# Layer 2's attention in a four-layer kernel: queries and context reordered by channel, parts cut, stored and loaded earlier

## What is computed

```python
qh = q.reshape(b * h, d // h, m)        # h = 8, d = 128, m = 256
kh = k.reshape(b * h, d // h, -1)
vh = v.reshape(b * h, c // h, -1)
qk = jnp.einsum('bdm,bdn->bmn', qh, kh) * scale
sm = jax.nn.softmax(qk, axis=-1)
ret = jnp.einsum('bmn,bcn->bcm', sm, vh)
...
x = x + _L2_xattn_ref(_layernorm(x, axis=-1), ctx_2048, ctx_2048)
```

## Time and profile before

| what | value |
|---|---|
| median of 3 runs | 2378.38 us (2377.53 to 2382.86) |
| the profiled execution's own time | 2386.57 us |
| its span | 2384.8 us |
| PE busy | 2021.2 us (85%) |
| DVE busy | 1812.9 us (76%) |
| ACT busy | 1405.9 us (59%) |
| POOL busy | 1170.7 us (49%) |

### The profile page before, as it was taken

How to read it: one execution, slowest core, us unless ns; L and a number is a source line. 1 busy time by engine, 2 the same in 40 slices (tenths; PEclk the granted TensorE clock), 3 DMA queues, 4 the chain that set the end, 5 groups by cost and what they waited for, 6 DMA issues and landing times.

```text
span 2384.8 us, 42664 instructions
## 1 busy us (share of the span) xinstructions
PE 2021.2 (85%) x13467; PEld 1235.8 (52%) x13467; DVE 1812.9 (76%) x4024; ACT 1405.9 (59%) x3555; POOL 1170.7 (49%) x1397
## 2 busy tenths in 40 slices
PE   5999879999589999999999995794687667888787
PEld 2444355666267677677777774462343233333245
DVE  4899658475589999999998877664785996888464
ACT  0677621453278888888888882231366563777543
POOL 3444100442678888888888762334762122334100
PEclk9999769999799999999999996897699675999789
DMA  5566420786310000000110004333994113777200
GB/s 139 142 173 173 117 78 8 244 246 203 70 33 19 21 19 21 17 21 19 21 21 17 3 1 180 122 87 106 221 249 137 53 32 79 178 183 184 67 14 27
DMA packets 258181, 223.19 MB, mean 94 GB/s; under 512 B 36585, under 2 KB 237900, under 8 KB 257708
## 3 DMA queue, kind: packets, MB, share of 16 engines
q1 hardware_dynamic: 234668, 178.72, 27.5%
q0 software_dynamic: 12240, 32.39, 5.5%
q10 hardware_dynamic: 11056, 9.38, 1.3%
HBM read 141.98 MB, written 79.32 MB: 93 GB/s over the span
## 4 chain that ended last, share of the span: by engine, by line
PE 58%; DVE 17%; POOL 10%; issue 7%; ACT 5%; DMA 2%; SPq 1%; POOLq 0%; ACTq 0%; DVEq 0%
PE bank L3216 8%; PE bank L713 5%; PE bank L691 4%; PE bank L1534 4%; PE bank L3176 3%; PE bank L3165 3%; PE bank L3209 3%; PE bank L1547 3%; PE bank L2113 3%; PE bank L3152 3%; PE bank L3144 2%; PE bank L3197 2%; POOL f_hr L3536 2%; PE bank L754 1%; POOL f_rows L3518 1%
## 5 line engine op out<-in xcount | busy, mean ns | idle before, releaser
L3216 PE MATMUL bank<-f_w,f_zc 128*128 128x512 bf16 x1152 | 283.8, 383 | 22.2 <-DVE f_zc L3324 18.1
L3536 POOL TENSOR_TENSOR f_hr<-f_hr,half_pow 128x4 f32<-128x4 f32 x192 | 244.9, 1275 | 84.3 <-DVE f_hr L3333 84.1
L926 ACT ACTIVATE a_PT<-bank 128x512 f32<-128x512 f32 x384 | 214.6, 603 | 82.6 <-PE bank L698 74.0
L815 DVE TENSOR_REDUCE a_nm<-bank 128x2 f32<-128x512 f32 x384 | 243.0, 683 | 21.1 <-PE bank L691 20.4
L3428 ACT ACTIVATE f_Pm<-bank,f_nmax 128x128 f32<-128x128 f32 x512 | 183.0, 383 | 73.6 <-DVE f_nmax L3348 73.4
L691 PE MATMUL bank<-a_stack_k,a_stack_q 57*128 57x256 bf16 (+1 forms) x768 | 165.1, 299 | 70.5 <-DVE a_nm L815 41.7
L3216 PEld LDWEIGHTS bank<-f_w,f_zc 128*128 128x128 bf16 x1152 | 112.4, 99 | 122.2 <-issue 25.1
L926 ACT ACTIVATE f_w<-bank 128x512 f32<-128x512 f32 x256 | 141.2, 599 | 48.6 <-PE bank L698 37.2
L815 DVE TENSOR_REDUCE f_w<-bank 128x2 f32<-128x512 f32 x256 | 162.4, 680 | 9.5 <-PE bank L691 8.0
L3343 DVE TENSOR_TENSOR f_raw<-bank,f_hr 128x512 f32<-128x512 f32 x192 | 131.5, 685 | 42.7 <-POOL f_hr L3536 42.7
L3525 POOL TENSOR_TENSOR f_cf<-f_cbr,f_cmr 128x516 f32<-128x516 bf16 x128 | 157.0, 1227 | 12.6 <-DVE f_cb L3373 11.0
(11 more groups left out here) (406 smaller groups left out, 5221.1 us busy)
## 6 DMA issues: line engine op xcount, KB each, us to landing
o<-a_sums SPq DMA_DIRECT2D x32, 512.0 KB
cut<-a_parts SPq DMA_DIRECT2D x64, 192.0 KB
cut<-a_parts SPq DMA_DIRECT2D x96, 128.0 KB
m_w<-in_w SPq DMA_DIRECT2D x32, 368.0 KB
moe_out<-m_oe ACTq DMA_DIRECT2D x32, 256.0 KB
cut<-f_w SPq DMA_DIRECT2D x32, 192.0 KB, 3.5
cut<-f_w SPq DMA_DIRECT2D x48, 128.0 KB, 2.6
f_w<-cut SPq DMA_DIRECT2D x32, 192.0 KB, 3.6
```

The lines of the kernel that those rows point to most:

```text
L815: v.tensor_reduce(self.nm[:, g % 2, :, at % self.J, at // self.J], self.k.bank[h % 3][:, :].rearrange("p (n m) -> p n m", n=2), AX.X, ALU. ...
L926: a.activation(self.PT[:, h % 8, :, :].rearrange("p m n -> p (m n)"), self.k.bank[3 + h % 3][:, :], ACT.Exp).then_inc(self.a_exp.sem, 1)
L3216: x = t.matmul(ps[:, :], self.zc[:, b % 2, j, c_, :], self.fp8.w3[:, m, c_, at:at + BANK], start=(m == 0 and c_ == 0), stop=(m == 2 and c_ ...
L3536: g.tensor_tensor(f, f, self.k.half_pow[:, 0:self.HPB], ALU.pow).then_inc(self.g_hr.sem, 1)
```

## The change

- The 128 channels of layer 2's attention are reordered, so that all eight heads of one channel index stand side by side (channel d of head h at row 8d + h instead of 16h + d). ctx comes in that order from a second input array. The queries are brought into it by a matmul with a permutation matrix `order_q` (`R`, step 8b+5), and ACT copies the result from bank 7 to `QK` (`copy_R`, step 8b+6). DVE now writes the normalised queries to `xn`. `copy_V` puts V back in order of heads.
- The DRAM tensor `cut` of layer 2 is laid out as part, channel, position. A row of a stack is then 4 KB without a gap. Four DMAs store an element's parts instead of five, and of k three part planes are stored instead of six. Four DMAs load the stacks instead of two.
- ACT's first part moves from step 8b+13 to 8b+7, POOL's cutting from 8b+14 to 8b+7, the store from 8b+19 to 8b+11, and the load of elements 0 to 5 from 8b+27 to 8b+14.
- POOL clears the first four buffers of V ahead of step 0. The gathers of element 2, which stood in step 0, follow the first cutting; the others keep their places.

```diff
+
+    def loaded(self, t):
+
+        b = self.starts(t, 14)
+        if self.layer == 2 and b is not None and b < self.NST:
+            return b
+        b = self.starts(t, 27)
+        return b if self.layer != 2 or b is not None and b >= self.NST else None
...
             yield "V", self.starts(t, 0)
+        if self.layer == 2 and self.starts(t, 5) is not None:
+            yield "R", self.starts(t, 5)
         if self.layer == 0 and self.starts(t, 6) is not None:
...
         self.stats, self.mv = s("stats", [P, B, 6]), s("mv", [P, B, 4])
-        self.cut = k.nc.dram_tensor(f"cut_{layer}", (B, 2, P, 6, D), BF16, kind="Internal").ap()
+        self.cut = k.nc.dram_tensor(f"cut_{layer}", (B, 2, P, 6, D) if layer != 2 else (B, 2, 6, P, D), BF16, kind="Internal").ap()
         self.o_out = k.nc.dram_tensor(f"o_{layer}", (B, heads, 32, D), F32, kind="Internal").ap()
...
         self.v_var, self.g_pow, self.v_x, self.a_V = (claim(f"a_{n}", B) for n in ("v_var", "g_pow", "v_x", "a_V"))
+        self.a_R = claim("a_a_R", B * (layer == 2))
         self.g_qk = claim("a_g_qk", 2 * B * (layer == 0))
...
         loads = []
+        if self.layer == 2:
+            rows = self.cut[b].rearrange("w c (d s) n -> w (c d) s n", d=self.hd)
+            loads.append((self.stack_q[0:self.ROWS, i, :, :], rows[0]))
+            for at, n in ((0, 3), (3, 2), (5, 1)):
+                loads.append((self.stack_k[at * self.hd:(at + n) * self.hd, i, :, :], rows[1, 0:n * self.hd]))
+            return loads
         for w, stack in enumerate((self.stack_q, self.stack_k)):
...
         A, layer = self.k.A, self.layer
+        if layer == 2:
+            sp.dma_start(self.order_q[:, :], A["c_order"]).then_inc(self.d_par.sem, 16)
         if layer == 0:
...
         dst = self.QK[:, i, 1, :] if self.layer == 2 else self.ctx_t[:, i, :]
-        sp.dma_start(dst, self.k.A["ctx"][:, b, :]).then_inc(self.d_ctx[i].sem, 16)
+        src = self.k.A["ctx_by_channel" if self.layer == 2 else "ctx"]
+        sp.dma_start(dst, src[:, b, :]).then_inc(self.d_ctx[i].sem, 16)
     def store_cut(self, sp, b):
+
         i, d = b % self.NB, self.d_cut[b % self.NB]
         sp.wait_ge(self.g_p2.sem, self.g_p2.at(b + 1))
+        if self.layer == 2:
+            for at, n, w, c_, m in ((0, 3, 0, 0, 1), (3, 2, 0, 1, 1), (5, 1, 0, 2, 1), (0, 3, 1, 0, 3)):
+                src = self.parts[:, i, w, c_:c_ + m, :]
+                src = src.to_broadcast([P, n, D]) if n > m else src
+                sp.dma_start(self.cut[b, w, at:at + n].rearrange("c p n -> p c n"), src).then_inc(d.sem, 16)
+            return
         q, kk = self.parts[:, i, 0], self.parts[:, i, 1]
...
                 t.wait_ge(self.a_V.sem, self.a_V.at(at + 1))
+            elif what == "R":
+                t.wait_ge(self.a_R.sem, self.a_R.at(at + 1))
             else:
...
             x.then_inc(self.p_m.sem, 1)
+        if what == "R":
+            if at == 0:
+                t.wait_ge(self.d_par.sem, self.d_par.at(1))
+            t.wait_ge(self.v_x.sem, self.v_x.at(at + 1))
+            t.matmul(ps[:, 0:D], self.order_q[:, :], self.xn[:, i, :], start=True, stop=True).then_inc(self.p_m.sem, 1)
         if what in "XCQ":
...
             v.wait_ge(self.g_pow.sem, self.g_pow.at(at + 1))
-            if at >= self.NB and layer == 2:
-                v.wait_ge(self.g_p2.sem, self.g_p2.at(at - self.NB + 1))
-            if at >= self.NB and layer != 2:
-                v.wait_ge(self.p_m.sem, self.p_m.at(self.uses["X" if layer == 0 else "Q", at - self.NB] + 1))
-            dst = self.QK[:, i, 0, :] if layer == 2 else self.xn[:, i, :]
-            v.tensor_scalar(dst, X[:, at, :], m[:, 0:1], m[:, 3:4], ALU.subtract, ALU.mult).then_inc(self.v_x.sem, 1)
+            if at >= self.NB:
+                v.wait_ge(self.p_m.sem, self.p_m.at(self.uses[{0: "X", 2: "R", 3: "Q"}[layer], at - self.NB] + 1))
+            v.tensor_scalar(self.xn[:, i, :], X[:, at, :], m[:, 0:1], m[:, 3:4], ALU.subtract, ALU.mult).then_inc(self.v_x.sem, 1)
         for w, what, after in ((1, "C", 7), (0, "X", 10)):
...
             self.copy_V(a, self.starts(t, 1))
-        if self.starts(t, 13) is not None:
-            self.first_part(a, self.starts(t, 13))
+        if self.layer == 2 and self.starts(t, 6) is not None:
+            self.copy_R(a, self.starts(t, 6))
+        if self.starts(t, self.FIRST) is not None:
+            self.first_part(a, self.starts(t, self.FIRST))
         q = self.quad(t - 1)
...
             a.wait_ge(self.p_O.sem, self.p_O.at((b - self.NV + 1) * self.heads // 4))
+        if self.layer == 2:
+            a.copy(self.V1[:, i, :, :, 0:self.hd], ps[:, 0:D].rearrange("p (n d h) -> p n h d", n=2, h=self.heads)).then_inc(self.a_V.sem, 1)
+            return
         if self.layer != 3:
...
+    def copy_R(self, a, b):
+        i = b % self.NB
+        a.wait_ge(self.p_m.sem, self.p_m.at(self.uses["R", b] + 1))
+        if b >= self.NB:
+            a.wait_ge(self.g_p2.sem, self.g_p2.at(b - self.NB + 1))
+        a.copy(self.QK[:, i, 0, :], self.k.bank[7][:, 0:D]).then_inc(self.a_R.sem, 1)
+
     def first_part(self, a, b):
         i = b % self.NB
         if self.layer == 0:
             a.wait_ge(self.g_qk.sem, self.g_qk.at(2 * b + 2))
         if self.layer == 2:
-            a.wait_ge(self.v_x.sem, self.v_x.at(b + 1))
+            a.wait_ge(self.a_R.sem, self.a_R.at(b + 1))
             a.wait_ge(self.d_ctx[i].sem, self.d_ctx[i].at(b // self.NB + 1))
         if self.layer == 3:
             a.wait_ge(self.v_m.sem, self.v_m.at(self.by_dve["Q", b] + 1))
         if b >= self.NB:
-            a.wait_ge(self.d_cut[i].sem, self.d_cut[i].at(5 * (b // self.NB)))
+            a.wait_ge(self.d_cut[i].sem, self.d_cut[i].at(self.n_cut * (b // self.NB)))
         a.copy(self.parts[:, i, :, 0, :], self.QK[:, i, :, :]).then_inc(self.a_p0.sem, 1)
...
             g.tensor_tensor(m[:, 3:4], m[:, 2:3], k.half_pow[:, 0:1], ALU.pow).then_inc(self.g_pow.sem, 1)
-            if at < self.NV:
+            if at < self.NV and not (self.pairs and at < self.SOON):
                 self.clear_V(g, at)
-            if self.pairs and at == 0:
-                self.pairs.gather(g, 2)
         for w, what, after in ((1, "C", 8), (0, "X", 11)):
             at = self.starts(t, after)
             if at is not None and layer == 0:
                 g.wait_ge(self.v_m.sem, self.v_m.at(self.by_dve[what, at] + 1))
                 x, y = self.QK[:, at % self.NB, w, :], self.t1[:, at % self.NB, w, :]
                 g.tensor_tensor(x, x, y, ALU.add).then_inc(self.g_qk.sem, 1)
-        at = self.starts(t, 14)
+        at = self.starts(t, self.PARTS)
         if at is not None:
...
                             ALU.subtract).then_inc(self.g_p2.sem, 1)
-        at = self.starts(t, 15)
-        if at is not None and self.pairs and at + 3 < B:
-            self.pairs.gather(g, at + 3)
+        at = self.starts(t, 7)
+        if at is not None and self.pairs and at + 2 < B:
+            self.pairs.gather(g, at + 2)
         at = self.ended(t, self.SUM + 2)
...
     g["mask"] = m.reshape(-1)
+    by_channel = np.arange(P).reshape(8, 16).T.reshape(-1)
+    g["ctx_by_channel"] = np.ascontiguousarray(g["ctx"][by_channel])
+    g["c_order"] = np.ascontiguousarray(np.eye(P, dtype=np.float32)[by_channel].T)
     g["mask_T"] = np.ascontiguousarray(m.reshape(B, DC, P).transpose(2, 0, 1))
     g.update(more_arrays(a))
     g.update(constants())
```

More of the change, by code:

```diff
@@ L335 @@
     LEAD, TURNED, EXP, VALUES, SUM = 40, 21, 22, 24, 53
-    HEAD_BANK = 5
+    HEAD_BANK, SOON = 5, 4
     def __init__(self, k, layer, pairs=None, headed=False, tailed=False):
@@ L351, in __init__ @@
         self.NB = 2 if layer != 2 else 4
+        self.FIRST, self.PARTS, self.CUT = (13, 14, 19) if layer != 2 else (7, 7, 11)
         self.ctx = ExitStack()
@@ L466, in allocate_head @@
             self.m_out = k.nc.dram_tensor("mask_rows", (B, 2, self.MROWS, D), BF16, kind="Internal").ap()
+        if layer == 2:
+            self.order_q = s("order_q", [P, P])
         self.signals()
@@ L471, in signals @@
         last = lambda name, n, unit=1: claim(f"tail_{name}" if self.tailed else f"a_{name}", n, unit, own=self.tailed)
-        self.n_load = {0: 5, 2: 0, 3: 5 + self.heads}[layer]
+        self.n_load = {0: 5, 2: 1, 3: 5 + self.heads}[layer]
+        self.n_cut = 5 if layer != 2 else 4
         self.n_stack = len(self.loads(0))
@@ L478, in signals @@
         self.d_ctx = [claim(f"a_d_ctx{i}", B // self.NB, 16) for i in range(self.NB)]
-        self.d_cut = [claim(f"a_d_cut{i}", B // self.NB * 5, 16) for i in range(self.NB)]
+        self.d_cut = [claim(f"a_d_cut{i}", B // self.NB * self.n_cut, 16) for i in range(self.NB)]
         self.d_stack = [claim(f"a_d_stack{i}", B // self.NB * self.n_stack, 16) for i in range(self.NB)]
@@ L562, in sp_step @@
     def sp_step(self, sp, t):
-        b = self.starts(t, 19)
+        b = self.starts(t, self.CUT)
         if b is not None:
```

(8 more changed lines are left out.)

## The result

The changed kernel takes 2415.14 us (median of 4 runs, 2412.84 to 2417.64), the kernel before 2380.62 beside it (4 runs, 2377.53 to 2383.39): ratio 1.0151, 95% interval 1.0130 to 1.0172, so it is slower by 34.5 us in the medians. (Ratios here are those on record with their intervals; a quotient of two medians, here 1.0145, can differ from them by about 0.001.) The forecast was slower by 18.7, 2397, with a range up to 2412, and 2415.14 lies above that range. The sign was right, the size too small.

What follows compares the result with a forecast made beforehand. The prediction took POOL's rounds, with their waits for ACT's cast, to bound layer 2's attention. It summed 1.9 + 11.2 + 6 + 4.7 - 1.1 - 4 = +18.7 us, giving 2397 against the median 2378.38, range 2380 to 2412.

Steps and rivals of the forecast that it cites:

- What bounds the stage: Layer 2's attention: its length is the sum of POOL's rounds until cutting ends; POOL waited 29.0 us for ACT's first part.
- Start, +1.9: Ahead of the first power: four clears of V, about 0.78 us each, move that power by +1.9 us.
- Lead-in, +11.2: Power 0 to power 5: rounds of 9.42 us with R in the chain, 47.6 us against 36.4, +11.2.
- Power 5 to 9, +6: Four rounds: R, its copy and handoffs add 1.8 us each; taken as +6 us, bounds +3 and +7.2.
- Power 9 to 14, +4.7: Five rounds: floor 10.0 us from 8.09 plus 1.9, taken as 10.4 against 9.46, +4.7 us, bounds 0 and +9.7.
- End of cutting: After power 14: only element 15's cutting is left behind, 20.9 us against 22.1, term -1.1 us.
- relief: DVE's waits for reloaded sums: larger rows and smaller stores shorten the DMA queue, -4 us, bounds 0 and -4.8.
- estimate of 2 us: Alternative for the DMA saving: fixed packet overhead gives only 14% of the loads' time, -2 us instead of -4.
- The signs: Expected: lead-in rounds 9.4 us, waits 2.9, first scores near 1683; wrong if middle rounds exceed 12 or sums' waits stay.
- Absorbed: Rival for the middle rounds: existing slack hides the new chain, which costs only in the lead-in; +10.2, 2389 us, chance 0.14.
- PE at its lower level in the middle: Rival: longer waits at R drop PE's clock, up to +19 over five rounds; +33, 2411 us, chance 0.13.
- The DMA queue sets the middle: Rival: transfers pace rounds 5 to 14, which fall to 8.1 us with R hidden; -7, 2371 us, chance 0.07.

Runs made afterwards that it cites:

- e4: The changed kernel with POOL's cutting at step 14, behind the next element's power, stores at 15, first loads at 20; cast stays at 7: 2357.97 us, ratio 0.9915.
- e8: The kernel before with ACT's cast of layer 2 at step 7 instead of 13, nothing else changed: 2362.23 us, ratio 0.9929.
- e2: The changed kernel without R and its copy, so the queries' channels stay unsorted; DVE writes the normalised queries to QK: 2389.1 us, ratio 1.0049.
- e5: The changed kernel with all nine clears of V ahead of the first power instead of four: 2409.32 us, ratio 1.0135.
- e6: The changed kernel itself, unaltered, run and profiled again: 2410.48 us, ratio 1.0143.
- e7: e3 with one number changed, ACT's cast at step 5 instead of 7: 2377.18 us, ratio 0.9996.
- e3: The kernel before (old layout, no R) with the new steps, including those of first loads, clears and gathers: 2392.07 us, ratio 1.0057.
- e10: The steps of e4 on the new layout without R and its copy, queries' channels left unsorted: 2358.55 us, ratio 0.9911.
- e9: The steps of e4 on the old layout (512-byte rows) without R: 2359.63 us, ratio 0.9920.

## Why the prediction was right or wrong

**What bounds the stage: right.** The stage follows POOL's rounds, and the wait for ACT's cast decides them: of the 26.0 us that the stage grew, POOL's waits for the cast are 20.9. e4 and e8 show it in the other direction: without the wait the stage falls by 25.4 and 17.6 us.

**Start, +1.9: measured +1.3.** The four clears took 2.57 us, 0.64 each, where I had taken 0.78. It is counted from the stage's first gather (1633.34 us to power 0 at 1640.81, 7.5 us; before, 1634.57 to 1640.74, 6.2), because the stage itself began 1.2 us earlier.

**Lead-in, +11.2: measured +10.5, right with its parts.** R took 1.19, its copy 0.37, the cast 0.62; the normalisation took 0.41 instead of 0.59. e2 puts R's share at 8.7 us of the five rounds, as priced.

**Power 5 to 9, +6: measured +9.4, beyond its bound of +7.2. This is the step that failed.** "The chain grows by R 1.22, copy 0.37 and about 0.2" took the new chain to be R's in every round. From the start of each power to the start of its own round's cutting, or before the change to that of the element before, POOL's timelines give, in us:

| round | 5 | 6 | 7 | 8 |
|---|---|---|---|---|
| before | 2.31 | 3.15 | 3.17 | 4.84 |
| after | 4.15 | 4.98 | 6.05 | 7.61 |
| growth | 1.84 | 1.83 | 2.88 | 2.77 |
| e2, without R | 2.33 | 4.17 | 5.54 | 6.73 |
| e5, clears ahead | 3.51 | 3.50 | 4.45 | 4.45 |

The growths add up to 9.3, the whole of the stretch's +9.4. In rounds 5 and 6 they are the 1.8 forecast, in round 6 partly by luck, since 1.0 of it is there without R. In 7 and 8, where exponentials run, they are 2.9 and 2.8, and without R the times are still 2.4 and 1.9 above those before. The longer chain there is clear, copy of V, exponentials, scores of the steps up to R, R, exponential, cast. As the cutting now stands behind the power of its own round, everything up to step 7 in three engines' programs must pass while POOL waits, with PE at a granted clock of 0.53 in 1700 to 1720. e5 removes one link and 6.9 us go; e2 removes R and 4.6 go. In round 7 ACT also loads a table, once. The cast stood ahead of that load in the kernel before and stands behind it now; the timelines of ACT before

```profile
1698.73 0.61 ACT L983 CAST a_parts<-a_QK 128x512 bf16<-128x512 f32 x1
1699.36 1.28 ACT L926 ACT_TABLE_LOAD   x1
```

and after

```profile
1713.35 1.28 ACT L963 ACT_TABLE_LOAD   x1
...
1716.13 0.61 ACT L1030 CAST a_parts<-a_QK 128x512 bf16<-128x512 f32 x1
```

How much of its 1.28 us lies on the chain no run separates.

**Power 9 to 14, +4.7: measured +5.9, near for a wrong reason.** The floor of 10.0 came from adding R's 1.9 to 8.09. Without R the rounds are the same (e2: 53.2 us). (e6's profile has 54.6, so the stretch is known to 1.4 us.) What counts is the step of the cast: two steps earlier, and 7.9 us go (e7 against e3). In the kernel before the cast stood at step 5 of a round (13 = 8 + 5), in the changed one at 7. I had one exponential more in the chain; it was the order of ACT's program as a whole that should have been counted.

**End of cutting and relief, -1.1 and -4: measured +0.3 together (-0.9 in e6's profile).** Where R is absent the stretch after power 14 gains 4.4 from e3 to e2. With R that was mostly taken back: e2 to the changed kernel +3.3 there (+2.1 with e6). DVE's waits for sums, where the relief of 4 was placed, fell by 2.0: 16.8 us before, 14.8 after. One of them in the changed kernel:

```profile
1817.62 0.43 DVE L922 TENSOR_TENSOR a_sums<-a_sums 128x256 f32<-128x256 f32 x1 [3.58 <-DMA a_sums<-r]
```

Why R costs anything in that stretch isn't settled; other profiles of it range from 67.1 (e6) to 68.7 (e5), and e4 and e10 differ by only 0.3 there. The size of 4 agrees with the 4.3 to 5.0 us that two pairs show in the stage, but that is luck, for the mechanism isn't shown: within these pairs DVE's waits for sums are 14.9 and 14.5 us (e3, e2) and 12.5 and 12.6 (e9, e10), so the gain came by another way, which stays open. The estimate of 2 us from the Trainium skill ("DMA: Bandwidth & Descriptors", Why small descriptors are slow) was below these pairs' stage times. The stores' smaller volume is in them too, and the medians (3.0 and 1.1) can't tell 2 from 4.

**The sum.** 1.3 + 10.5 + 9.4 + 5.9 + 0.3 = 27.4 us in the stage, 8.7 more than forecast. The medians show 34.5 and 31.5. The rest, 4 to 7 us, has no place in the stage; the lower ends of the two intervals are 31 and 27. A profiled execution's time less the stage (here from its first gather on) is 2184 and 2190 us for the two of the changed kernel, but 2188 for the one of the kernel before, and 2179 to 2188 for the others with either layout. So executions differ outside the stage by more than the rest, and whether the change costs something there stays open. (Two slips in the forecast's sums are of 0.1 us: the total with the page's estimate is 20.7, not 20.8, and 22.1 less 20.9 is 1.2, not 1.1.)

**The signs.** Lead-in rounds, their waits, power 5 (10.6 us later, 11.8 from the stage's first gather, for 13) and the first scores (1680.39 for 1683) came near what was forecast. Two of the signs of being wrong came as well: rounds 7 and 8 with 12.75 and 14.32 us, above 12, and the sums' waits, which mostly stayed.

**The rivals.** *Absorbed* fell, although its idea was right for R in the late middle. *PE at its lower level in the middle* came partly: 0.53 in 1700 to 1720, where before had 0.61, then 0.81, where before had 1.00, and up to 1.00 later. It goes with the waits (e4, without them, has 1.00 in the same window); what it adds to them no run separates. *The DMA queue sets the middle* fell: the old layout ran rounds of 7.2 to 8.2 us from power 5 to 12, at up to 309 GB/s (e9). The rule on early issue and late waits that spoke for it (the Trainium skill, "DMA: Bandwidth & Descriptors", Rules for kernel authors) was followed only by half: the change issued transfers early by making POOL wait at once for its inputs, and the new steps alone cost 14.5 us of the stage (e3).

## What to carry to other kernels

When a step is moved in hand-ordered programs, count the steps of every engine between the event that starts the round and the one awaited, not only the new instructions on the data's path: two steps of ACT's program were worth 14.9 us here, and a new matmul with its copy 1.7 us a round where nothing else stood in the chain, and nothing where other steps did. Produce an input early and consume it behind the next round's first instruction: one number (e8) made the old kernel 0.7% faster, and the changed kernel with its cutting there (e4) is 0.85% faster than the old. The saving in transfers was at most 5 us of the stage, with or without such waits, and nearly too small for the medians.

## What was unexpected of the hardware

DMA share 1.0 was no ceiling: the kernel before had 1.00 at 245 GB/s and 1.09 at 270 GB/s, and the same layout moved 309 GB/s at 1.07 in e9. Of DVE's two equal additions of a pair's rows, the first took 0.48 us and the second, as POOL's cutting ran beside it, 1.32; here in the lead-in of the changed kernel:

```profile
1653.04 0.48 DVE L1953 SCALAR_TENSOR_TENSOR X<-pair_rows,pair_pr,X 128x256 f32<-128x256 f32 x1 [2.07 <-DMA pair_rows<-top_out,pair_place]
1653.56 1.32 DVE L1955 SCALAR_TENSOR_TENSOR X<-pair_rows,pair_pr,X 128x256 f32<-128x256 f32 x1
```

This is the rule and not a chance: 11 of the 32 additions in the changed kernel began while one of the cutting's two 128x512 TENSOR_TENSORs was running on POOL, and each of them ended 0.27 to 0.29 us after POOL's did, 0.72 to 1.40 us long. Most that began first kept their 0.48 us. With the cutting behind the power (e4) only three began so. POOL's cutting can thus delay DVE in a second way, besides the wait for the power. What they share there, no run here tells.
